# A two-block transformer kernel: three written step tables laid out in another order

## The reference

```python
# layer 0
h = layernorm(x) * (1 + ca) + sa;  x = x + ga * attn0(h)      # 16 heads of 16, blocks of 64 tokens
h = layernorm(x) * (1 + cb) + sb;  x = x + gb * coupling(h)   # three cycles of a small net
# coupling: out = h; three times:
#   out = out + (0.1 + r * (0.7*g + 0.3*net(out) - 0.5) * 2) * twist(out)   net: 256-256-128-64-1
# layer 1
h = layernorm(x) * (1 + ca) + sa;  x = x + ga * attn1(h)      # 8 heads of 64, causal
#   scores = qc@kc.T - silu((qc@vu.T) @ sigmoid(qu@ku.T).T);  out = softmax(scores) @ vc
h = layernorm(x) * (1 + cb) + sb;  x = x + gb * experts(h)    # 8 experts choose 128 tokens each
```

## Time and profile before

| what | value |
| --- | --- |
| median of 3 runs | 1942.31 us (1942.08 to 1942.38) |
| span of the profiled execution | 1941.7 us |
| PE busy | 1911.9 us (98%) |
| VectorE busy | 1093.9 us (56%) |
| ScalarE busy | 919.0 us (47%) |
| GpSimd busy | 694.8 us (36%) |

### The profile page before, as it was taken

How to read it: one execution, slowest core, us unless ns; L and a number is a source line. 1 busy time by engine, 2 the same in 40 slices (tenths; PEclk the granted TensorE clock), 3 DMA queues, 4 the chain that set the end, 5 groups by cost and what they waited for, 6 DMA issues and landing times.

```text
span 1941.7 us, 30308 instructions
## 1 busy us (share of the span) xinstructions
PE 1911.9 (98%) x11192; PEld 1317.8 (68%) x11192; DVE 1093.9 (56%) x2904; ACT 919.0 (47%) x1970; POOL 694.8 (36%) x769
## 2 busy tenths in 40 slices
PE   8989999999999999999999999999999999999998
PEld 5835655765575666557656655665786888888887
DVE  5767676558556746656585655577534447223221
ACT  5646666556565555655665566454334321111111
POOL 3302334334332433252343324343443433333332
PEclk9989999999999999999999999999999999999999
DMA  3020001000000100010001000050130223333333
GB/s 129 2 87 15 12 1 39 1 23 12 28 23 1 39 1 23 1 39 15 9 13 28 13 10 15 23 176 2 31 85 4 59 73 98 66 76 79 85 76 70
DMA packets 59696, 76.78 MB, mean 40 GB/s; under 512 B 7120, under 2 KB 52824, under 8 KB 59296
## 3 DMA queue, kind: packets, MB, share of 16 engines
q1 hardware_dynamic: 46448, 57.28, 8.9%
q0 software_dynamic: 12288, 16.79, 5.0%
q10 hardware_dynamic: 816, 0.79, 0.1%
HBM read 53.71 MB, written 21.00 MB: 38 GB/s over the span
## 4 chain that ended last, share of the span: by engine, by line
PE 96%; DVE 2%; ACT 1%; DMA 0%; issue 0%; POOL 0%; SPq 0%; ACTq 0%; DVEq 0%; POOLq 0%
PE bank L765 15%; PE bank L982 12%; PE bank L995 11%; PE bank L832 7%; PE bank L887 4%; PE bank L856 4%; PE bank L868 4%; PE bank L781 3%; PE bank L750 3%; PE bank L591 3%; PE bank L900 3%; PE bank L617 3%; PE bank L841 3%; PE bank L712 2%; PE bank L818 2%; PE bank L692 2%
## 5 line engine op out<-in xcount | busy, mean ns | idle before, releaser
L1232 ACT ACTIVATE h<-bank 128x512 f32<-128x512 f32 x128 | 76.3, 597 | 363.9 <-PE bank L982 352.8
L982 PE MATMUL bank<-xin,ew 128*128 128x256 f32 x1024 | 234.3, 381 | 0.0
L995 PE MATMUL bank<-ew,h 128*128 128x256 f32 x1024 | 226.7, 379 | 0.0
L1776 POOL TENSOR_TENSOR s<-s,ri 128x256 f32<-128x256 f32 (+3 forms) x128 | 160.0, 1268 | 156.5 <-DVE ri L1531 156.5
L995 PEld LDWEIGHTS bank<-ew,h 128*128 128x128 f32 x1024 | 194.2, 190 | 27.7 <-issue 1.5
L982 PEld LDWEIGHTS bank<-xin,ew 128*128 128x128 f32 x1024 | 189.5, 190 | 23.4 <-issue 0.2
L1814 POOL DMA_INDIRECT out<-y,indices x64 | 104.2, 1628 | 265.9 <-DVE y L1668 164.9
L1208 ACT ACTIVATE s<-s,mn 128x128 f32<-128x128 f32 (+3 forms) x256 | 141.0, 552 | 109.0 <-DVE mn L1524 108.9
L1509 DVE SCALAR_TENSOR_TENSOR th<-th,bank 128x384 f32<-128x384 f32 (+1 forms) x192 | 104.3, 594 | 112.0 <-ACT th L1199 110.6
L1668 DVE SCALAR_TENSOR_TENSOR y<-bank,gates,gbe 128x256 f32<-128x256 f32 x64 | 31.0, 484 | 238.5 <-PE bank L995 230.1
L832 PE MATMUL bank<-look,term 128*128 128x384 f32 (+3 forms) x512 | 152.7, 438 | 0.0
(11 more groups left out here) (320 smaller groups left out, 3641.3 us busy)
## 6 DMA issues: line engine op xcount, KB each, us to landing
ew<-L_ffn_w SPq DMA_DIRECT2D x24, 1024.0 KB
x1s<-x_scratch SPq DMA_DIRECT2D x8, 512.0 KB
out<-x1s SPq DMA_DIRECT2D x8, 512.0 KB, 2.9
xn_scratch<-n_xn SPq DMA_DIRECT2D x8, 512.0 KB, 2.9
x<-L_attn_x SPq DMA_DIRECT2D x7, 512.0 KB, 3.8
x_scratch<-x SPq DMA_DIRECT2D x7, 512.0 KB, 3.0
wqkv<-w_qkv SPq DMA_DIRECT2D x1, 3072.0 KB, 10.7
wqkv<-L_wmod SPq DMA_DIRECT2D x2, 1024.0 KB, 8.0
```

What stands on the lines that cost most here:

```text
L982: mm = te.matmul(banks[i][:, g * 2 * P:(g + 1) * 2 * P], w1[:, kk, (2 * n + g) * P:(2 * n + g + 1) * P], xin[:, kk, :, :].rearrange("p h s ...
L995: mm = te.matmul(banks[i][:, 0:D], ex.h1[:, g, n * P:(n + 1) * P], w2[:, g, :], start=(g == 0), stop=(g == FC - 1))
L1776: done = g.tensor_tensor(sc, sc, b1.ri[u % 2][:, m, :].unsqueeze(2).to_broadcast([P, 2, w]), ALU.mult)
```

## The change

Only the texts of HEAD, PERIOD and LAST are written anew. The set of steps, all buffers, and the code of each step with its waits stay. What differs is where each engine has each step, which bank a product falls into, and with it which earlier product a matmul waits for. A line or two of each table as the diff has it:

```diff
 HEAD = """
-    0stats:0 0silu:0 1stats:0 0wqkv_load:0 0mod_load:0 0x0:0 0norm:0 1norm:0 0cols:0 0setup:0 1x0:0 0mod_load:1
+    0stats:0 0silu:0 0norm:0 1stats:0 1x0:0 0mod_load:0 0x0:0 1norm:0 0mod_load:1 0w0_load:0 0cols:0 0cols:1
...
 PERIOD = """
-    proj:0.0 +x0:0 proj:0.2 +stats:0 +norm:0 proj:0.3 +ga0_load:0 proj:0.1 proj:1.4 +feat:0 -attend:10 look:0.0
+    proj:0.3 proj:0.1 proj:0.0 +ga0_load:0 +x0:0 +feat:0 proj:1.3 +stats:0 +bias0:0 +norm:0 proj:0.2 +kq:0 -weigh:11
```

More of the change, by code:

```diff
@@ L58 @@
[L58 to L67, removed]
@@ new lines @@
+    0wqkv_load:0 0feat:0 0rows:0 0setup:0 1feat:0 0kq:0 0kq:1 0v:0 0setup0:0 0sc0:0 0sc0:1 1silu:0 1kq:1 1mod_load:1
+    0wt0:0 0wt0:1 1kq:0 0sc0:2 0sc0:3 0tp0:0 0tp0:1 0wt0:2 0bias0:0 1sc0:0 0v:1 1sc0:1 0wt0:3 1wt0:0 0pv0:0 1wt0:1
+    1mod_load:0 0sc0:4 0tp0:2 0tp0:3 0sc0:5 0wt0:4 0ga0_load:0 1sc0:2 0wt0:5 1tp0:0 0sc0:6 0pv0:1 1sc0:3 0tp0:4 0tp0:5
+    1bias0:0 1tp0:1 0sc0:7 1v:1 0pv0:2 1ga0_load:0 0w1_load:0 1v:0 0tp0:7 0tp0:6 0wt0:6 1tp0:2 0wt0:7 1wt0:2 1wt0:3
+    1sc0:4 1pv0:0 0pv0:3 1wt0:4 1sc0:5 1tp0:3 1cols:0 1wt0:5 1sc0:6 1tp0:4 1sc0:7 1wt0:6 2ga0_load:0 1wt0:7 1pv0:1
@@ L77 @@
+    0su:9 0attend:6 0sw:9 0turn:7 2norm:2 0proj:3.4 0weigh:8 0su:10 0sw:10 0w:3.1 0attend:7 0sc:9 0sc:10 0turn:8
+    0weigh:9 0weigh:10 1feat:2 0su:11 0sw:11 0attend:8 0o_out:2 0turn:9 2feat:2 0attend:9 0sc:11 0turn:10
 """
 PERIOD = """
-    proj:0.0 +x0:0 proj:0.2 +stats:0 +norm:0 proj:0.3 +ga0_load:0 proj:0.1 proj:1.4 +feat:0 -attend:10 look:0.0
-    +bias0:0 look:0.1 look:0.2 term:0 +kq:0 -x1_load:0 +kq:1 turn_vu:0 -weigh:11 proj:1.0 +sc0:0 +sc0:1 proj:1.2
-    +wt0:0 +wt0:1 -turn:11 proj:1.1 +tp0:0 proj:0.4 +sc0:2 +tp0:1 +sc0:3 +v:0 +wt0:2 +v:1 w:0.0 w:0.1 -attend:11
@@ L85 @@
[L85 to L94, removed]
@@ L95 @@
-    sw:10 sc:10 su:11 turn:9 weigh:10 sw:11 sc:11 attend:9 +feat:2 turn:10
+    proj:0.3 proj:0.1 proj:0.0 +ga0_load:0 +x0:0 +feat:0 proj:1.3 +stats:0 +bias0:0 +norm:0 proj:0.2 +kq:0 -weigh:11
+    +kq:1 look:0.0 look:0.1 look:0.2 term:0 +v:1 +v:0 -attend:10 -x1_load:0 +sc0:0 proj:1.4 +wt0:0 +sc0:1 proj:1.1
+    turn_vu:0 +wt0:1 -turn:11 +tp0:0 +sc0:2 proj:1.2 proj:1.0 +tp0:1 +wt0:2 +sc0:3 +tp0:2 proj:0.4 +wt0:3 +sc0:4 +pv0:0
+    w:0.0 -attend:11 +tp0:3 +sc0:5 su:0 su:1 sw:0 +wt0:4 -o_out:3 sw:1 sc:0 +pv0:1 w:0.1 weigh:0 +wt0:5 +sc0:6 -out1:0
@@ new lines @@
+    -out1:1 turn_vu:1 +tp0:4 vc:1 turn:0 vc:3 +sc0:7 -stats_t:0 +tp0:5 su:2 +wt0:6 vc:0 +wt0:7 sw:2 +pv0:2 +tp0:6 +tp0:7
+    look:1.0 -norm_t:0 sc:2 sc:1 look:1.1 term:1 look:1.2 attend:0 w:1.0 +pv0:3 proj:2.1 +out0:0 +out0:1 su:3 su:4 vc:2
+    +stats:1 +norm:1 proj:2.2 weigh:1 sw:3 sw:4 proj:2.0 turn:1 +feat:1 weigh:2 sc:3 attend:1 weigh:3 -feat_t:0 +gc:0
+    turn:2 +cn1:0 sc:4 look:2.0 attend:2 turn:3 -gate:0 +cn2:0 +twist:0 weigh:4 +cn3:0 +gc:1 o_out:0 w:1.1 +gc:2 +cn4:0
+    proj:2.4 look:2.1 turn_vu:2 +cn1:1 proj:2.3 su:5 +cn2:1 sw:5 attend:3 +cn3:1 sc:5 w:2.0 term:2 turn:4 +cn4:1
@@ L96 @@
+    proj:3.2 proj:3.3 -softmax:0 su:6 su:7 +cn1:2 sw:6 sw:7 w:2.1 +cn2:2 attend:4 -probs:0 +cn3:2 weigh:5 sc:6 +cn4:2
+    look:2.2 proj:3.4 proj:3.0 proj:3.1 turn_vu:3 weigh:6 sc:7 turn:5 su:8 +gate0:0 sw:8 look:3.0 weigh:7 attend:5
+    o_out:1 turn:6 sc:8 term:3 look:3.1 w:3.0 weigh:8 attend:6 turn:7 +fin0:0 su:9 sw:9 attend:7 look:3.2 +stats:2 sc:9
+    turn:8 su:10 w:3.1 weigh:9 sw:10 o_out:2 sc:10 attend:8 su:11 +norm:2 weigh:10 turn:9 sw:11 sc:11 attend:9 turn:10
+    +feat:2
 """
 LAST = """
-    7x0:0 7stats:0 5proj:0.0 5proj:0.1 5proj:0.4 5proj:0.3 7norm:0 7ga0_load:0 5proj:0.2 7feat:0 7bias0:0 5turn_vu:0
@@ new lines @@
+    5sc:4 7twist:0 7gc:2 7cn4:0 5weigh:4 5look:2.1 5proj:2.3 7cn1:1 5su:5 5x1_load:0 5sw:5 5look:2.2 5proj:3.1 5proj:2.2
+    7cn2:1 5turn_vu:2 5turn:3 4gate:0 5sc:5 5term:2 7cn3:1 5attend:3 5proj:3.0 5turn:4 5w:2.0 5w:2.1 5su:6 5weigh:5
+    5sw:6 7cn4:1 5su:7 7cn1:2 5attend:4 5proj:3.3 5sw:7 5turn:5 5proj:2.4 5su:8 5sc:6 5sw:8 5proj:3.4 5proj:3.2
+    5attend:5 5look:3.0 5look:3.1 5sc:7 5look:3.2 5term:3 5weigh:6 5turn_vu:3 5o_out:1 7cn2:2 6proj:0.0 4softmax:0
+    5w:3.0 5sc:8 5turn:6 6proj:0.3 5su:9 5weigh:7 7cn3:2 5weigh:8 5w:3.1 5attend:6 6proj:0.4 5sw:9 6proj:0.2 5turn:7
@@ new lines @@
+    6proj:0.1 5attend:7 5sc:9 5su:10 5turn:8 6turn_vu:0 5weigh:9 5sw:10 5su:11 5o_out:2 5attend:8 6look:0.0 5sw:11
+    6term:0 6look:0.1 6look:0.2 5sc:10 5weigh:10 4probs:0 5turn:9 6proj:1.1 6proj:1.2 6w:0.0 5sc:11 6w:0.1 5attend:9
+    5weigh:11 7cn4:2 6proj:1.0 6turn_vu:1 5turn:10 6proj:1.3 6su:0 6sw:0 6look:1.0 6su:1 6sc:0 6sw:1 6su:2 5attend:10
+    6sw:2 6proj:1.4 7gate0:0 5turn:11 6weigh:0 6sc:1 6look:1.1 6look:1.2 6w:1.0 5attend:11 5o_out:3 6term:1 6vc:2
+    5out1:0 6vc:3 6vc:0 5out1:1 6turn:0 6proj:2.1 6su:3 6vc:1 6weigh:1 5stats_t:0 6sw:3 6sc:2 6proj:2.0 6su:4 6sw:4
@@ new lines @@
+    6attend:11 7sw:1 6o_out:3 7sc:0 7look:1.1 7vc:0 6out1:0 experts 7weigh:0 7su:2 7sw:2 7look:1.2 7sc:1 experts*2
+    7proj:2.0 7vc:2 7vc:1 7turn_vu:1 7weigh:1 experts 7turn:0 experts 7vc:3 7w:1.0 experts 7w:1.1 7attend:0 7sc:2
+    7weigh:2 7term:1 7proj:2.1 6out1:1 experts 7turn:1 experts 7su:4 7su:3 experts 7sw:3 7look:2.0 7sw:4 experts
+    7attend:1 experts*4 6stats_t:0 experts 7proj:2.2 experts 7turn:2 experts 7look:2.1 7sc:3 experts*2 6norm_t:0
+    experts*5 7su:5 7weigh:3 experts 7sw:5 7look:2.2 7sc:4 7o_out:0 7attend:2 experts 7turn:3 7proj:2.3 experts 7weigh:4
```

100 lines of the change are left out of this document (44 added, 56 removed).

## The result

The changed kernel takes 1964.87 us (median of 4 runs, 1963.54 to 1970.21) against 1942.19 us before. The ratio is 1.0124, 95% interval 1.0109 to 1.0138: slower by 1.1 to 1.4%. The profiled execution has a span of 1962.4 us (20.7 more than before's) and a time of 1963.79 us.

The account below looks back on a forecast made before the run. PE was taken as the bound, busy 1911.9 of 1941.7 us. Terms 15 + 3.5 + 2 + 2 - 2 - 1.5 = +19.0 gave 1960.7, plus 0.6 from span to median: 1961 us, range 1941 to 1972.

Parts of the forecast that it names:

- Edges between shapes (+15): Whole order on PE: 81 more changes of array shape, at 0.15 to 0.20 us each, add about 15 us.
- The split by kind in the prediction: Added shape changes: 41 into 64 rows (8.2 us), 18 into 64 columns (2.7), 8 (1.6) and 16 (2.6) to 128.
- The rival by which edges are free: Shape changes cost nothing in their new places; the sum is +3.9, about 1946 us; chance 0.12.
- PE's busy time: Over the whole kernel, PE's busy time must grow by about 15 us with the same matmuls.
- The boundary (+3.5): At three PERIOD ends, feat behind three proj instead of five waits 1.15 us for the norm: +3.5 us.
- The start (+2): Batch 0's x is transferred fourth instead of third, so PE's first matmul starts later: +2 us, bounds 0 and +3.
- Only 0.47 us of this vanishes in a later wait: At the start, a later wait for the weights' second part absorbs only 0.47 us of PE's delay.
- cn2 and cn3 (+2): In 87 to 147 us, they become neighbours in two more cycles of batch 2, so PE waits for ACT: +2 us.
- The norm (-2): Near 87 us, earlier bias0 on GpSimd no longer runs beside batch 0's second-half norm, 1.38 instead of 3.88: -2 us.
- The waits that go (-1.5): PE's recurring wait of sc behind th, 1.5 us in 7 times, is laid out otherwise: -1.5 us.
- Table loads (0): ACT's 16 more table loads, 20.5 us, fit into its idle time and cost nothing.
- Faster by the head's half-clock stretches: Rival: between 87 and 147 us a better mix keeps PE busy, and up to 23 us come back; chance 0.10.

Follow-up runs that it names:

- the appended groups: Kernel before with extra four-matmul groups in three array shapes appended at TensorE's end, pure then mixed; 0.19, 0.17 and 0.16 us for each change of shape.
- HEAD alone: Kernel before with only its HEAD table replaced by the changed kernel's; 1949.62 us, ratio 1.0036.

## Why the prediction came out as it did

The forecast was 1961 (range 1941 to 1972, slower), the result 1964.9. The direction and the main mechanism were right; the smaller terms of the head and the count of the boundaries were mis-sized, and several waits weren't seen. The sum is nearer than its parts, and that is luck. In the profiled execution PE's idle time grew by 10.6 us, where the wait terms (3.5 + 2 + 2 - 2 - 1.5) make 4; its busy time grew by 10.1, where 15 were forecast.

**Edges between shapes (+15).** Shown. The price of 0.15 to 0.20 us was read from equal groups with other neighbours, and holds both alone (0.16 to 0.19) and in the kernel (0.175). 81 edges at 0.175 are 14.2 us, the largest part of the 20.7: 1.6 in each period, and 6.0 of LAST's 7.1. (The split by kind in the prediction has two slips that nearly cancel: 16 edges at 0.15 are 2.4, not 2.6, and its kinds make 83, since two edges at the 8-column matmuls went away.) The rival by which edges are free would have given 1946; the run with nothing but 13 more edges in each period excludes it. Where the Trainium skill's page "TensorEngine Tiling (Array Packing)", section "Key Properties", says that a change of tiling mode drains TensorE, this case agrees as far as it shows a cost at each such change, 0.16 to 0.19 us in the appended groups. That a drain makes it isn't shown.

**PE's busy time** grew by 10.1, not 15. An edge's price is all busy time (the run with 52 more edges has 9.0 us more), so 14 us were due. Up to 147 us this execution has 4.9 us less than before's for the same 705 recorded matmuls, with the higher clock from 87 us on, and that is the difference.

**The boundary (+3.5).** Price right (1.15 forecast, 1.04 measured), count wrong: I left out the boundary at HEAD's end, where the first PERIOD begins with the same three proj. Four times 1.04 are 4.2, and the run with feat one proj later takes them away. The list of waits shows 0.26 to 0.30 us of each; the rest lies inside the groups.

**The period as a whole.** 9 edges at 0.175 are 1.6, the boundary 1.04, tp0's wait 0.5 of excess from start to start, and the gone wait of sc -0.4 (also from start to start; the list has 0.2 of it): 2.7, where 2.63 was measured. The wait of tp0 is in no step of the prediction. From the timeline of PE after the change:

```profile
575.06 0.63 PE L625 MATMUL bank<-ident,s0a 128*128 128x128 f32 x4
576.06 0.63 PE L625 MATMUL bank<-ident,s0a 128*128 128x128 f32 x4 [0.38 <-POOL s0a L1722]
```

Four transposes wait 0.38 us for the GpSimd product of the previous softmax, in each period.

**The start (+2).** The first matmul came at 12.0, where about 11 was forecast, and the step "Only 0.47 us of this vanishes in a later wait" failed. I looked for the next wait on PE's list alone; in the run with only the transfers moved, feat is 1.9 us late, and at the first sc0 0.4 are left, with +1.1 us at the end (interval -0.4 to +3.1). After the change 1.6 are left at that place.

**cn2 and cn3 (+2).** The mechanism is right. Both new waits are there, and have the 0.78 of the earlier trace rows, so 1.6 us together:

```profile
264.88 0.65 PE L720 MATMUL bank<-a2a,cw 128*64 128x256 f32 x4 [0.78 <-ACT a2a L1145]
...
283.58 0.65 PE L720 MATMUL bank<-a2a,cw 128*64 128x256 f32 x4 [0.78 <-ACT a2a L1145]
```

A third new one, again 0.78, stands at 104.88, where the kernel before had other work; I hadn't seen it.

**The norm (-2).** The row is as forecast (1.38), but the step from the row to PE failed: I took the norm's 2.5 us as PE's, and PE waited 1.32 us for it. By itself the move is worth 1.0 us in the medians, with an interval that reaches to nothing, and 1.7 where it was added to the order with fewer edges (1942.99 to 1941.31). In the same stretch the wait for the later norm, at 143.68 before, grew from 2.97 to 4.26 us, which no term has.

**The waits that go (-1.5).** They went, and tp0's came.

**HEAD as a whole.** My terms for it (11 edges, start, cn, norm) made +4. The changed kernel's trace says +3.0 at the first PERIOD, the one of HEAD alone +6.5, and the runs with HEAD alone +7.7 (4.5 to 9.5). The traces divide it at batch 0's first proj. From there to the first PERIOD (from:to and length, busy time by engine, PEclk), before and with HEAD alone:

```profile
146.96:323.35 176.39, 175.42 (x1024) 103.99 (x1025) 125.67 (x292) 110.98 (x238) 62.56 (x73) 0.98 0.05 17
...
149.41:329.86 180.45, 177.09 (x1027) 103.44 (x1026) 126.59 (x292) 113.92 (x241) 64.16 (x73) 0.99 0.05 16
```

The stretch takes 180.09, 180.45 and 180.76 us in the three profiled executions with the changed HEAD, and 175.65 to 176.39 in all eleven with before's or a variant of it, at a granted clock of 0.98 to 1.00. So about 4 us are order: 12 more edges (2.1 at the price above), the two cn3 waits (1.6), and a new wait of cn1 (L691) of 1.0 us for VectorE, less the gone wait of sc. Up to batch 0's first proj the clock blurs the rest: with before's HEAD (seven executions) this proj came between 144.5 and 147.0, in four variants of it between 140.4 and 143.8, and in the three with the changed HEAD at 146.3, 149.4 and 151.7, with granted clocks from 0.78 to 0.91 between 87 and 147 us. The changed kernel's runs spread over 6.7 us. How much of the remaining 3 to 4 us is order and how much clock stays open; I have no run that holds the clock fixed.

**Table loads (0).** No row ties a wait of PE to one of the 16 more loads, and the period closes to 0.1 us without them. A run that takes only them away wasn't made.

**Faster by the head's half-clock stretches.** The clock of that stretch did rise to 0.91, but the time of it wasn't won: batch 0's first proj came 0.7 us earlier, not 20. PE still stood idle for 11.3 of these 60 us. That the serial chain keeps it so is argued; no run shows it.

## What to carry to other kernels

When TensorE is busy nearly all of the time, its busy time isn't a constant of the work: count the changes of array shape in the order of issue, price them from equal groups with different neighbours in the trace, and only then look for waits. An order that keeps 64-row and 64-column work in runs is worth about 0.175 us for each change saved, but every step that is moved for it must still find its operand ready and its PSUM bank drained. In this well balanced order most of the saving came back as waits. Some of them the list of PE's waits doesn't show, since they lie inside a group; look at the weight loads there. And what a slow instruction costs is the wait of the engine that needs it, not its own excess. Compare period lengths in the trace, since nearly all repeat to 0.01 us, and not only medians, in which the start-up phase's clock moves by several us.
